# Layer 3 cross-attention: the order in which each unit's turns, score groups and sums are issued, and VectorE's order with it

## The chip, the cores and the metric

One core of a Trainium2 chip runs the whole program. The metric is the device time of one execution in microseconds (us): the kernel before has a median of 3372.61 us over 3 runs (3367.91 to 3373.32).

## The reference, cut to what matters

The program is a four-layer perceiver with 128 latent rows of width 256. The change touches one stage, the cross-attention of layer 3, whose main part is attention of 16 heads over all but the last 4 of 12,544 context rows of width 192:

```python
q = _split_heads(q_in)
k = _split_heads(k_in)
v = _split_heads(v_in)
s = jnp.einsum('bhid,bhjd->bhij', q, k) * SCALE
p = jax.nn.softmax(s, axis=-1)
o = jnp.einsum('bhij,bhjd->bhid', p, v)
```

## The kernel before, in words

The stage never builds keys or values. The key weights are folded into the queries, so a score is a product of a folded query (128 rows by 192) with a raw context row, and the softmax's weighted sum is taken over raw context rows; the value weights are applied afterwards by `finish_absorbed`. Each number is split into a high and a low fp32r part, so one product is several matmuls.

`absorbed_cross_attention` (line 1581) goes through 7 chunks of 1792 context rows, and in each through 16 heads: 112 **units** (`NU`), `u = 16 * chunk + head`. A unit has these steps:

- `raw_scores(u, s)`, s = 0 to 3 (lines 1607 to 1618), on TensorE: five matmuls of 448 columns (L1613 to L1617) into PSUM bank s % 2. The last signals `raw`. Two banks serve all groups, so group s waits (line 1611) for `maxed`, the end of VectorE's `keep` of the group two before.
- `keep(u, s)` (line 1694) on VectorE: L1701 copies the 448 scores out of PSUM into `raw[u % 2]`, with their maximum; the profile shows it as two instructions, the second reading the accumulator. It signals `maxed`.
- `new_max(u)` (line 1707) on VectorE: L1711 takes the maximum and signals `negmax`, L1715 stores it.
- `exp(u)` (line 1655) on ScalarE: two exponentials of 896 columns in place (L1661), each signalling `probs`, and the old sum's factor (L1663).
- `turn(u, gr)`, gr = 0, 1 (line 1620), on TensorE: seven 128x128 transposes (L1625) of a half into its own two PSUM banks. It waits for `probs` and signals `turned`.
- `keep_high(u, gr)` (L1669) on ScalarE copies a turned half rounded to fp32r; `keep_low(u, gr)` (L1720) on VectorE subtracts it from the turned half and signals `low`.
- `sums(u, gr)` (line 1629) on TensorE: fourteen matmuls (L1637 and L1638 in turn) against the context rows, into bank 6 or 7. It waits (line 1630) for `low` of its half.
- `take(u)` (L1726, L1729) on VectorE adds the unit's sums to the running ones, scaled by the factor.

Each engine's queue is in order and written out by hand. TensorE's order (lines 1642 to 1651) is, for each unit u: turn(u, 0), scores (u+1, 0) and (u+1, 1), turn(u, 1), scores (u+1, 2) and (u+1, 3), sums(u, 0), sums(u, 1). VectorE's (lines 1738 to 1747) is: keep_low(u, 0), keep(u+1, 0), keep(u+1, 1), take(u-1), keep_low(u, 1), keep(u+1, 2), keep(u+1, 3), new_max(u+1). ScalarE's is: keep_high(u, 0), keep_high(u, 1), exp(u+1). GpSimd splits the next chunk's context rows once per chunk and SyncE loads them; both are one chunk ahead.

Of the kernel before, what the change touches and what calls it, by code (L numbers as in the profile page):

```python
# [56 lines left out]
class Stage:  # L57
# [5 lines left out]
    def sem(self, name):  # L63
        if name not in self.sems:
            self.sems[name] = self.nc.alloc_semaphore(f"{self.tag}_{name}")
        return self.sems[name]
# [18 lines left out]
def at_least(eng, sem, value):  # L85

    if isinstance(value, int) and value <= 0:
        return
    eng.wait_ge(sem, value)
# [19 lines left out]
def bank(g, n, lo=0, hi=BANK):  # L109
    return g.ps[:, n * BANK + lo:n * BANK + hi]  # L110
# [1470 lines left out]
def absorbed_cross_attention(nc, g, a):  # L1581

    with ExitStack() as ctx:
# [9 lines left out]
        NU = NCH * H  # L1593

        def turned_banks(gr):
            return g.ps[:, (2 + 2 * gr) * BANK:(2 + 2 * gr) * BANK + GW]

        @block.sync
        def _(sp):
            for c in range(1, NCH):  # L1600
                if c >= 2:
                    sp.wait_ge(sem("split"), 6 * (c - 1))
                load_chunk(sp, g, a, c, sem("chunk"))

        @block.tensor
        def _(pe):
            def raw_scores(u, s):
                c, h = u // H, u % H
                if h == 0 and s == 0 and c > 0:
                    pe.wait_ge(sem("split"), 6 * c)  # L1610
                at_least(pe, sem("maxed"), 4 * u + s - 1)
                out, cols, p = bank(g, s % 2, 0, SUB), slice(s * SUB, s * SUB + SUB), c % 2
                pe.matmul(out, g.q_high[:, h, 0, :], g.high_a[:, p, cols], start=True, stop=False)  # L1613
                pe.matmul(out, g.q_high[:, h, 0, :], g.low_a[:, p, cols], start=False, stop=False)
                pe.matmul(out, g.q_low[:, h, 0, :], g.high_a[:, p, cols], start=False, stop=False)
                pe.matmul(out, g.q_high[:, h, 1, :], g.both_b[:, p, cols], start=False, stop=False)
                pe.matmul(out, g.q_low[:, h, 1, :], g.both_b[:, p, cols], start=False, stop=True)\  # L1617
                  .then_inc(sem("raw"), 1)

            def turn(u, gr):  # L1620
                pe.wait_ge(sem("probs"), 2 * u + gr + 1)
                at_least(pe, sem("low"), 2 * (u - 1) + gr + 1)
                for t in range(GT):
                    key = (gr * GT + t) * 128
                    last = pe.transpose(turned_banks(gr)[:, t * 128:t * 128 + 128], raw[u % 2][:, key:key + 128],  # L1625
                                        g.ident)
                last.then_inc(sem("turned"), 1)

            def sums(u, gr):
                pe.wait_ge(sem("low"), 2 * u + gr + 1)  # L1630
                if gr == 0:
                    at_least(pe, sem("taken"), u - 1)
                out = bank(g, 6 + u % 2, 0, TW)
                for t in range(GT):
                    tile, cols = gr * GT + t, slice(t * 128, t * 128 + 128)
                    rhs = g.tokens[:, u // H % 2, tile, :]
                    pe.matmul(out, high[gr][:, cols], rhs, start=(tile == 0), stop=False, skip_group_check=True)  # L1637
                    last = pe.matmul(out[:, 0:C + 2], low[gr][:, cols], rhs[:, 0:C + 2], start=False,  # L1638
                                     stop=(tile == TPC - 1), skip_group_check=True)
                last.then_inc(sem("sums"), 1)  # L1640

            for s in range(4):
                raw_scores(0, s)
            for u in range(NU):
                for gr in range(2):
                    turn(u, gr)
                    if u + 1 < NU:
                        raw_scores(u + 1, 2 * gr)
                        raw_scores(u + 1, 2 * gr + 1)
                sums(u, 0)  # L1650
                sums(u, 1)

# [39 lines left out]
        @block.vector  # L1692
        def _(dve):
            def keep(u, s):
                c, h = u // H, u % H
                last_keys = c == NCH - 1 and s == 3
                dve.wait_ge(sem("raw"), 4 * u + s + 1)
                if s == 0:
                    at_least(dve, sem("turned"), 2 * (u - 1))
                width = SUB - (IPA if last_keys else 0)  # L1700
                dve.tensor_scalar(raw[u % 2][:, s * SUB:s * SUB + width], bank(g, s % 2, 0, width), 0.0, None,  # L1701
                                  ALU.add, ALU.max, accum_out=tops[:, h, s:s + 1]).then_inc(sem("maxed"), 1)
                if last_keys:

                    dve.memset(raw[u % 2][:, CH - IPA:CH], -3e38)

            def new_max(u):
                c, h = u // H, u % H
                dve.wait_ge(sem("maxed"), 4 * u + 4)
                at_least(dve, sem("probs"), 2 * (u - 3))  # L1710
                dve.tensor_reduce(negmax[:, u % 4:u % 4 + 1], tops[:, h, :], AX.X, ALU.max, negate=True)\  # L1711
                   .then_inc(sem("negmax"), 1)
                dve.wait_ge(sem("negmax"), u + 1)
                old = 4 + (c + 1) % 2
                dve.tensor_scalar(tops[:, h, old:old + 1], negmax[:, u % 4:u % 4 + 1], -1.0, None, ALU.mult)\  # L1715
                   .then_inc(sem("top_kept"), 1)

            def keep_low(u, gr):
                dve.wait_ge(sem("high"), 2 * u + gr + 1)
                dve.tensor_tensor(low[gr][:], turned_banks(gr), high[gr][:], ALU.subtract).then_inc(sem("low"), 1)  # L1720

            def take(u):
                h, part = u % H, bank(g, 6 + u % 2, 0, TW)
                dve.wait_ge(sem("sums"), 2 * (u + 1))
                dve.wait_ge(sem("factor"), u + 1)
                dve.scalar_tensor_tensor(out=acc[:, h, :], in0=acc[:, h, :], scalar=factor[:, u % 4:u % 4 + 1],  # L1726
                                         in1=part[:, 0:CW], op0=ALU.mult, op1=ALU.add).then_inc(sem("scaled"), 1)
                dve.wait_ge(sem("scaled"), u + 1)
                dve.tensor_tensor(acc[:, h, 0:C], acc[:, h, 0:C], part[:, C + 2:TW], ALU.add)\  # L1729
                   .then_inc(sem("taken"), 1)  # L1730

            dve.memset(tops[:], -3e38).then_inc(sem("tops"), 1)
            dve.wait_ge(sem("tops"), 1)
            dve.wait_ge(sem("acc_zero"), 1)
            for s in range(4):
                keep(0, s)
            new_max(0)
            for u in range(NU):
                for gr in range(2):
                    keep_low(u, gr)  # L1740
                    if u + 1 < NU:
                        keep(u + 1, 2 * gr)
                        keep(u + 1, 2 * gr + 1)
                    if gr == 0 and u > 0:
                        take(u - 1)
                if u + 1 < NU:
                    new_max(u + 1)
            take(NU - 1)


# [1140 lines left out]
```

## Time and profile before

| | us |
|---|---|
| median of 3 runs | 3372.61 |
| the profiled execution | 3372.62 |
| its span in the trace | 3370.9 |

Over the whole span TensorE's matmuls are busy 2945.2 us (87%), VectorE 1830.0 us (54%), ScalarE 1350.9 us (40%). The units run from 2097 us to 3191 us of the span. In the trace PE is TensorE's matmuls and PEld its weight loads, which run beside them; DVE is VectorE and ACT is ScalarE. A line of the timeline gives the start, the duration, the engine, the line of the kernel, and how many like instructions were merged (x7: seven). A matmul's end is modelled and reaches past the start of the next, so TensorE's time is best read from start to start.

### The profile page before, as it was taken

The page shows a single profiled execution, that of the slowest core. Times are in us where ns is not written, and L with a number is a line of the kernel's source. Part 1 is how long each engine was busy: PE and PEld are TensorE (multiplying, and loading weights), DVE is VectorE, ACT ScalarE, POOL GpSimd, SP SyncE. Part 2 cuts the span into 40 slices and gives each one's busy share as a digit, 9 for nine tenths or more (in the row PEclk, how much of TensorE's full clock was granted, in tenths as well). Part 3 has the DMA queues.
Part 4 walks back from the last instruction along what each step waited for, and adds up shares of the span by engine and source line. Part 5 has one row for each costly group of instructions (what it writes and reads, how often), then busy time and mean ns, then how long its engine had stood idle before and what let it go on. Part 6 is the DMA issues. An engine that isn't in the chain of part 4 may idle for free. (4 is left out here: it accounts for less than half of the span.)

```text
span 3370.9 us, 66496 instructions
## 1 busy us (share of the span) xinstructions
PE 2945.2 (87%) x27158; PEld 2487.7 (74%) x27158; DVE 1830.0 (54%) x3246; ACT 1350.9 (40%) x2191; POOL 404.1 (12%) x571
## 2 busy tenths in 40 slices
PE   6999809998768999477999669999999999999978
PEld 6888706776564777463777455999999999999867
DVE  5555418774527775446776343555555555555524
ACT  4444305665003666123667120444444444444311
POOL 2443400000100000000000002220202020200000
PEclk9999958998787999686999685999999999999969
DMA  4898879882468883158884271100101010000016
GB/s 154 281 289 270 269 152 182 177 176 64 153 187 177 174 176 78 46 191 178 175 176 101 82 220 36 52 18 22 39 1 39 1 39 1 1 1 1 17 50 227
DMA packets 251093, 393.95 MB, mean 117 GB/s; under 512 B 45827, under 2 KB 214149, under 8 KB 250789
## 3 DMA queue, kind: packets, MB, share of 16 engines
q1 hardware_dynamic: 250791, 389.70, 45.3%
q8 instruction: 217, 3.56, 0.5%
q14 instruction: 85, 0.69, 0.1%
HBM read 289.45 MB, written 99.49 MB: 115 GB/s over the span
## 5 line engine op out<-in xcount | busy, mean ns | idle before, releaser
L712 DVE TENSOR_REDUCE L_xattn_tops<-psum 128x1 f32<-128x896 f32 x672 | 702.4, 1086 | 270.3 <-PE psum L564 269.1
L625 ACT ACTIVATE L_xattn_probs<-psum 128x512 f32<-128x512 f32 x1176 | 612.3, 600 | 518.2 <-PE psum L575 518.1
L1720 DVE TENSOR_TENSOR L_units_low<-psum,L_units_high 128x896 fp32r<-128x896 f32 x224 | 243.6, 1088 | 486.8 <-ACT L_units_high L1669 486.8
L564 PE MATMUL psum<-L_xattn_keys,L_xattn_q_stack 96*128 96x448 bf16 (+1 forms) x1344 | 395.2, 378 | 110.5 <-DMA L_xattn_q_stack<-query_parts 65.2
L1637 PE MATMUL psum<-wide_tokens,L_units_high 128*128 128x386 f32 x1568 | 456.5, 358 | 1.4 <-DVE L_units_low L1720 1.4
L575 PEld LDWEIGHTS psum<-L_xattn_q_stack,L_xattn_keys 99*128 99x128 bf16 (+1 forms) x4704 | 323.1, 98 | 144.4 <-issue 19.2
L575 PE MATMUL psum<-L_xattn_q_stack,L_xattn_keys 99*128 99x128 bf16 (+1 forms) x4704 | 394.2, 221 | 5.0 <-ACT L_xattn_probs L625 5.0
L1638 PE MATMUL psum<-wide_tokens,L_units_low 128*128 128x194 f32 x1568 | 395.1, 252 | 0.0
L588 PE MATMUL psum<-L_xattn_probs,L_xattn_values 128*17 128x128 f32 x9408 | 358.5, 277 | 0.2 <-issue 0.2
L1669 ACT CAST L_units_high<-psum 128x896 fp32r<-128x896 f32 x224 | 203.3, 908 | 363.7 <-PE psum L1625 363.7
L1661 ACT ACTIVATE L_units_raw<-L_units_raw,L_units_negmax 128x896 f32<-128x896 f32 x224 | 221.6, 1036 | 308.4 <-DVE L_units_negmax L1711 308.4
L1638 PEld LDWEIGHTS psum<-wide_tokens,L_units_low 128*128 128x128 f32 x1568 | 299.1, 191 | 1.7
L1637 PEld LDWEIGHTS psum<-wide_tokens,L_units_high 128*128 128x128 f32 x1568 | 294.9, 188 | 3.0 <-DVE L_units_low L1720 1.6
L588 PEld LDWEIGHTS psum<-L_xattn_probs,L_xattn_values 128*17 128x17 f32 x9408 | 260.7, 98 | 38.8 <-issue 1.1
L1701 DVE TENSOR_SCALAR_CACHE_REDUCE L_units_raw<-psum 128x448 f32<-128x448 f32 x448 | 259.7, 617 | 4.5 <-POOL wide_acc L1680 2.6
L564 PEld LDWEIGHTS psum<-L_xattn_keys,L_xattn_q_stack 96*128 96x128 bf16 (+1 forms) x1344 | 91.7, 100 | 220.9 <-issue 67.1
L1625 PE MATMUL psum<-band,L_units_raw 128*128 128x128 f32 x1568 | 207.9, 272 | 2.0 <-ACT L_units_raw L1661 2.0
L410 POOL TENSOR_TENSOR proj_parts<-proj_rest,proj_parts 128x896 bf16<-128x896 f32 x84 | 160.3, 1909 | 249.8 <-ACT proj_parts L328 249.8
L1625 PEld LDWEIGHTS psum<-band,L_units_raw 128*128 128x128 f32 x1568 | 179.9, 140 | 10.3 <-ACT L_units_raw L1661 2.4
L1613 PE MATMUL psum<-wide_high_a,wide_q_high 128*128 128x448 f32 x448 | 184.7, 412 | 2.2 <-PEq L78 2.2
L2578 PE MATMUL psum<-xnT,L_ffn_w 128*128 128x128 f32 x1056 | 141.3, 292 | 27.5 <-DMA L_ffn_w<-in_L_ffn_W 14.2
L2578 PEld LDWEIGHTS psum<-xnT,L_ffn_w 128*128 128x128 f32 x1056 | 137.3, 206 | 35.8 <-issue 14.2
(436 smaller groups left out, 3990.6 us busy)
## 6 DMA issues: line engine op xcount, KB each, us to landing
key_parts<-proj_parts SPq DMA_DIRECT2D x84, 672.0 KB, 5.1
L_xattn_keys<-key_parts SPq DMA_DIRECT2D x144, 336.0 KB, 4.7
values_scratch<-proj_values SPq DMA_DIRECT2D x18, 1904.0 KB, 11.9
L_xattn_values<-values_scratch SPq DMA_DIRECT2D x144, 238.0 KB, 5.4
L_ffn_w<-in_L_ffn_W SPq DMA_DIRECT2D x32, 1024.0 KB, 6.8
L_xattn_keys<-key_parts SPq DMA_DIRECT2D x144, 224.0 KB, 5.0
L_xattn_keys<-key_parts SPq DMA_DIRECT2D x192, 112.0 KB, 5.1
L_ffn_w<-in_L_ffn_w SPq DMA_DIRECT2D x16, 1024.0 KB, 6.3
```

The source lines that it names most:

```text
L564: last = pe.matmul(top_slot(n)[:, s, :], q_stack[0:P1, h, :], keys[0:P1, v % RING, key:key + WIN // 2], start=True, stop=True)
L575: last = pe.matmul(score_bank(k)[:, i * 128:i * 128 + 128], keys[0:P2, u % RING, key:key + 128], q_stack[0:P2, u // NCH, :], start=True, s ...
L588: last = pe.matmul(sum_bank[row:row + VW, :], values[:, u % RING, t, :], probs[:, at:at + 128], start=(c * TPC + t < 4), stop=(c * TPC + t ...
L625: act.activation(group_probs(k), score_bank(k), ACT.Exp).then_inc(sem("probs"), 1)
L712: dve.tensor_reduce(tops[:, h % 2, 2 * c + w:2 * c + w + 1], top_slot(n), AX.XY, ALU.max)\
L1625: last = pe.transpose(turned_banks(gr)[:, t * 128:t * 128 + 128], raw[u % 2][:, key:key + 128], g.ident)
L1637: pe.matmul(out, high[gr][:, cols], rhs, start=(tile == 0), stop=False, skip_group_check=True)
L1638: last = pe.matmul(out[:, 0:C + 2], low[gr][:, cols], rhs[:, 0:C + 2], start=False, stop=(tile == TPC - 1), skip_group_check=True)
L1661: act.activation(half, half, ACT.Exp, bias=new).then_inc(sem("probs"), 1)
L1701: dve.tensor_scalar(raw[u % 2][:, s * SUB:s * SUB + width], bank(g, s % 2, 0, width), 0.0, None, ALU.add, ALU.max, accum_out=tops[:, h, s: ...
L1720: dve.tensor_tensor(low[gr][:], turned_banks(gr), high[gr][:], ALU.subtract).then_inc(sem("low"), 1)
L2578: last = pe.matmul(bank(g, 2 * slot + half, j * T, j * T + T), buf[par][:, k, col:col + 128], g.xnT[:, k, :], start=(k == 0), stop=(k == D ...
```

## The change

TensorE issues both turns of unit u, then the four score groups of unit u+1, then the sums. VectorE's queue becomes: keep(u+1, 0), keep(u+1, 1), keep_low(u, 0), keep(u+1, 2), keep_low(u, 1), keep(u+1, 3), new_max(u+1), take(u-1). No instruction is added, removed or altered; the waits inside the steps stay as they are.

```diff
             for s in range(4):
                 raw_scores(0, s)
             for u in range(NU):
-                for gr in range(2):
-                    turn(u, gr)
-                    if u + 1 < NU:
-                        raw_scores(u + 1, 2 * gr)
-                        raw_scores(u + 1, 2 * gr + 1)
+                turn(u, 0)
+                turn(u, 1)
+                if u + 1 < NU:
+                    for s in range(4):
+                        raw_scores(u + 1, s)
                 sums(u, 0)
                 sums(u, 1)
...
             new_max(0)
             for u in range(NU):
-                for gr in range(2):
-                    keep_low(u, gr)
-                    if u + 1 < NU:
-                        keep(u + 1, 2 * gr)
-                        keep(u + 1, 2 * gr + 1)
-                    if gr == 0 and u > 0:
-                        take(u - 1)
-                if u + 1 < NU:
+                ahead = u + 1 < NU
+                if ahead:
+                    keep(u + 1, 0)
+                    keep(u + 1, 1)
+                keep_low(u, 0)
+                if ahead:
+                    keep(u + 1, 2)
+                keep_low(u, 1)
+                if ahead:
+                    keep(u + 1, 3)
                     new_max(u + 1)
+                if u > 0:
+                    take(u - 1)
             take(NU - 1)
```

## Rows read from the trace of the kernel before

**Rows 1.** The page's slices of the span: the granted TensorE clock in tenths.
```profile
PEclk9999958998787999686999685999999999999969
```

**Rows 2.** One stretch, from unit 0's first ScalarE copy to unit 111's: busy time by engine.
```profile
core 0: us, PE busy (x) PEld busy (x) DVE busy (x) ACT busy (x) POOL busy (x), PEclk, DMA share, GB/s
2106.81:3184.90 1078.09, 1078.09 (x6884) 1029.75 (x6883) 582.88 (x1568) 441.52 (x557) 116.43 (x36) 1.00 0.06 17
```

**Rows 3.** L1613, the first matmul of a score group, over all units: durations, count, starts.
```profile
L1613 PE MATMUL psum<-wide_high_a,wide_q_high x444: 360/406/477, 2106.5 to 3178.9; 128*128 128x448 f32 x148
```

**Rows 4.** Timeline of the matmuls through one unit, to the next unit's first turn.
```profile
2620.61 0.93 PE L1625 MATMUL psum<-band,L_units_raw 128*128 128x128 f32 x7
2621.29 0.45 PE L1613 MATMUL psum<-wide_high_a,wide_q_high 128*128 128x448 f32 x1
2621.58 0.36 PE L1614 MATMUL psum<-wide_low_a,wide_q_high 128*128 128x448 f32 x1
...
2622.18 0.36 PE L1617 MATMUL psum<-wide_both_b,wide_q_low 128*128 128x448 f32 x1
2622.38 0.36 PE L1613 MATMUL psum<-wide_high_a,wide_q_high 128*128 128x448 f32 x1
...
2623.38 0.93 PE L1625 MATMUL psum<-band,L_units_raw 128*128 128x128 f32 x7
2624.20 0.48 PE L1613 MATMUL psum<-wide_high_a,wide_q_high 128*128 128x448 f32 x1
2624.51 0.36 PE L1614 MATMUL psum<-wide_low_a,wide_q_high 128*128 128x448 f32 x1
...
2626.31 0.34 PE L1637 MATMUL psum<-wide_tokens,L_units_high 128*128 128x386 f32 x1
...
2630.32 0.93 PE L1625 MATMUL psum<-band,L_units_raw 128*128 128x128 f32 x7
```

**Rows 5.** Timeline of the weight loads of the same unit.
```profile
2621.26 0.19 PEld L1613 LDWEIGHTS psum<-wide_high_a,wide_q_high 128*128 128x128 f32 x1
2621.37 0.19 PEld L1614 LDWEIGHTS psum<-wide_low_a,wide_q_high 128*128 128x128 f32 x1
...
2622.18 0.19 PEld L1613 LDWEIGHTS psum<-wide_high_a,wide_q_high 128*128 128x128 f32 x1
...
2624.20 0.19 PEld L1613 LDWEIGHTS psum<-wide_high_a,wide_q_high 128*128 128x128 f32 x1
2624.30 0.19 PEld L1614 LDWEIGHTS psum<-wide_low_a,wide_q_high 128*128 128x128 f32 x1
```

**Rows 6.** Timeline of VectorE through the same unit.
```profile
2622.51 1.09 DVE L1720 TENSOR_TENSOR L_units_low<-psum,L_units_high 128x896 fp32r<-128x896 f32 x1 [4.34 <-ACT L_units_high L1669]
2623.52 0.61 DVE L1701 TENSOR_SCALAR_CACHE_REDUCE L_units_raw<-psum 128x448 f32<-128x448 f32 x1
2624.06 0.08 DVE L1701 DVE_READ_ACCUMULATOR L_units_raw<-psum 128x1 f32 x1
...
2624.60 0.41 DVE L1726 SCALAR_TENSOR_TENSOR wide_acc<-wide_acc,L_units_factor,psum 128x193 f32<-128x193 f32 x1
...
2626.86 0.62 DVE L1701 TENSOR_SCALAR_CACHE_REDUCE L_units_raw<-psum 128x448 f32<-128x448 f32 x1
...
2627.53 0.16 DVE L1711 TENSOR_REDUCE L_units_negmax<-L_units_tops 128x1 f32<-128x6 f32 x1
```

**Rows 7.** Timeline of ScalarE in the same unit.
```profile
2621.57 0.91 ACT L1669 CAST L_units_high<-psum 128x896 fp32r<-128x896 f32 x1 [1.39 <-PE psum L1625]
...
2627.72 1.98 ACT L1661 ACTIVATE L_units_raw<-L_units_raw,L_units_negmax 128x896 f32<-128x896 f32 x2 [2.46 <-DVE L_units_negmax L1711]
```

**Rows 8.** Timeline before the first unit, where VectorE waits for a score group.
```profile
2102.43 0.37 PE L1617 MATMUL psum<-wide_both_b,wide_q_low 128*128 128x448 f32 x1
...
2102.83 0.62 DVE L1701 TENSOR_SCALAR_CACHE_REDUCE L_units_raw<-psum 128x448 f32<-128x448 f32 x1 [0.80 <-PE psum L1617]
```

**Rows 9.** Timeline of the last unit, which has no score groups between its turns.
```profile
3183.93 1.70 PE L1625 MATMUL psum<-band,L_units_raw 128*128 128x128 f32 x14
...
3185.83 1.09 DVE L1720 TENSOR_TENSOR L_units_low<-psum,L_units_high 128x896 fp32r<-128x896 f32 x1 [4.37 <-ACT L_units_high L1669]
...
3186.98 0.44 PE L1637 MATMUL psum<-wide_tokens,L_units_high 128*128 128x386 f32 x1 [1.35 <-DVE L_units_low L1720]
```

## The prediction

> **What bounds the kernel now.** I read the page's slices first: the granted clock is 9 tenths or more through the slices that hold the units [rows 1], and the stretch from the first to the last unit has a granted clock of 1.00, the upper of the two levels, with TensorE busy for all of its 1078.09 us while VectorE is busy 582.88 and ScalarE 441.52 [rows 2]. So TensorE's queue sets the time, and no clock change is to be had. That stretch holds 111 periods: 1078.09 / 111 = 9.71 us a unit. A busy share of 100% says nothing of stalls, since matmul ends are modelled and cover small gaps; those are found in the timeline, from start to start. Every unit but the last issues four score groups for its successor, and the 444 first matmuls of such groups [rows 3] are 111 x 4.
>
> One unit on TensorE [rows 4]: from the first turn to the second 2.77 us, from the second turn to the sums 2.93, the sums 4.01, together 9.71. The two first pieces hold the same work, seven transposes and two score groups. A score group's five matmuls take 1.00: from L1614 to the next group's L1613, four matmuls on, are 0.80 (2621.58 to 2622.38), so 0.20 each. The first piece is therefore 0.77 + 2.00, the second 0.77 + 2.00 + **0.16 of stall**. The cause is in the queues: VectorE starts keep(u+1, 0) only behind keep_low(u, 0), which waits for ScalarE's copy; keep's accumulator read ends at 2624.06 + 0.08 = 2624.14 [rows 6], and the weight load of the third score group, which needs that PSUM bank, starts 0.06 later, at 2624.20 [rows 5]. In the undisturbed first piece this load comes 0.65 after the turn's first matmul (2621.26 against 2620.61), so it was due at 2624.03 and came 0.17 late. The same 0.06 between VectorE's end and TensorE's start stands in the last unit (3185.83 + 1.09 = 3186.92, then 3186.98) [rows 9].
>
> **The change, part by part.** I put T at the first turn's first matmul and work out the new unit.
>
> *TensorE.* The same instructions in another order. Fourteen transposes in one stretch are in the last unit already: 1.70 against 0.93 for seven, so the second seven cost 0.77 [rows 4, 9], as above; no switching cost disappears or appears. Scores 4 x 1.00, sums 4.01. Without stalls: 1.54 + 4.00 + 4.01 = 9.55 us. Score group 2's first matmul (L1613) is due at T + 0.77 + 2.77 = T + 3.54, group 3's at T + 4.54, the first sum at T + 5.54. The gain is the stall, 0.16, if nothing takes its place. What was freely early before now must be checked, because keep(u+1, 0), keep(u+1, 1) and keep_low(u, 0) each gate TensorE directly.
>
> *Gate 1, keep(u+1, 0) before score group 2.* The group's last matmul, L1617, starts 1.57 after its turn's first matmul [rows 4], so at T + 0.77 + 1.57 = T + 2.34. VectorE starts 0.40 after it when it is waiting (2102.43 to 2102.83) [rows 8], T + 2.74; the accumulator read ends 0.62 later (2623.52 to 2624.14) [rows 6], and with 0.06 the weight load is released at T + 3.42. Undisturbed it would go 0.20 before its matmul (2622.18 against 2622.38) [rows 4, 5], at T + 3.34. So it is 0.08 late. How much of that reaches the matmuls depends on how long a load needs: behind the stall, the next load starts 0.10 after the released one, and its matmul L1614 stands 0.31 after it, that is 0.10 of load and 0.20 of matmul [rows 4, 5]. A load released at T + 3.42 is ready at T + 3.52, before T + 3.54. Bounds: 0 lost (the load hides under the running matmul) and 0.08 (none of the lateness hides). I take 0, because the row with the 0.10 is the same load of the same line.
>
> *Gate 2, keep(u+1, 1) before group 3.* All of it is 1.00 later, so it loses nothing beyond gate 1.
>
> *Gate 3, keep_low(u, 0) before the sums.* It was done 2.7 us before the first sum (2622.51 + 1.09 = 2623.60, against 2626.31) [rows 4, 6]; now it is queued behind two keeps. keep(u+1, 1) starts at T + 3.74, the next VectorE instruction 0.54 after it (as 2623.52, 2624.06 and 2624.60) [rows 6], keep_low lasts 1.09 and with 0.06 the sums' load is released at T + 5.43, ready at T + 5.53; the sum is due at T + 5.54. A subtraction right behind a keep isn't in the trace. Below, its pitch is 0.54 as for the next keep and for take's first instruction; above, 0.67 as for L1711 (2626.86 to 2627.53), which waits on the keep itself [rows 6]. I take 0.54, since keep_low needs nothing of the keep. With 0.67 the sums come 0.12 late. Gates are absolute times, so the losses don't add: the unit loses the largest one.
>
> *The rest of the ring.* keep(u+1, 2) starts 1.01 behind keep_low's start (2622.51 to 2623.52), T + 5.29; keep_low(u, 1) at T + 5.83, released for sums(u, 1) at T + 6.98, due T + 7.35; keep(u+1, 3) T + 6.84; new_max 0.67 later; ScalarE's exponentials 0.19 behind that (2627.53 to 2627.72), T + 7.70, and 1.98 long [rows 6, 7]. With 0.06 the second turn is released at T + 9.74 and its load is due at T + 10.21: 0.47 to spare, 0.67 for the first turn. ScalarE's copies start 0.96 behind each turn's first matmul [rows 4, 7], so the first is ready at T + 1.87 and the second at about T + 2.7, before VectorE asks for either. take(u-1), moved to the end, fits the idle time from T + 7.9 to T + 12.3, and the sums it takes are complete shortly after T; its `taken` is next needed by sums(u+1, 0) at T + 15. Cost nothing. GpSimd and SyncE keep their waits on counts that TensorE reaches no later, and no transfer moves.
>
> *Ends.* Unit 111 has no scores, so both orders run alike; unit 0's second turn waits some 0.2 us for its exponential once.
>
> *Sum.* 111 x 0.16 = 17.8 us, less 0.2, less an allowance of 0.01 a unit for gates with a margin of 0.01 to 0.02 (1.1 us): 16.5. The profiled execution, 3372.62, is within 0.01 of the median. 3372.6 - 16.5 = **3356.1 us**, 0.5% faster.
>
> **A rule that speaks against it.** The Trainium skill (TensorE: Matmul & The Clock Gate, "The mechanism" under "Part 3: Packing small matmuls — row/col tiling") says that weight loads overlap matmuls in flight only where their row groups differ. Here every matmul uses all 128 rows; by that rule a late load would delay its matmul in full, and the result would be the first rival's 3364.8. The trace disagrees so far: loads start 0.20 before their own matmuls, beside the one before, and a pitch of 0.20 for 448 columns leaves no room for a serial 0.10.
>
> **The rivals.**
>
> *Late loads are passed on (chance 0.15).* The unit loses 0.08 to 0.09 of the 0.16; 111 x 0.07 = 7.8 us remain: **3364.8**. For it: three gates lie within 0.02 us of my limit, and one pitch is taken from another instruction. Against it: the 0.10 of the released load.
>
> *The stall comes back in full (0.10).* Either a released load starts only when the running matmul has drained (group 1's L1617 at T + 3.34 with a modelled 0.36, so the next at T + 3.70 in place of 3.54), or keep_low's pitch is 0.67 and a little more. Both cost 0.12 to 0.17 a unit: **3372.6**, no change. The stall of before doesn't exclude the first, since there the load began as the transposes ended.
>
> *VectorE's queue becomes the bound (0.04).* The place is keep_low(u, 0), behind two keeps and ahead of the sums. It decides from 0.17 us of further delay (0.16 of gain and the margin of 0.01), and can be measured as slower from 0.06 beyond. If the subtraction's pitch were doubled to 1.08, the sums would come 0.53 late: 111 x 0.37 = 41 us slower, **3414**. Against it: no VectorE row shows a pitch longer than the instruction itself by more than 0.06.
>
> *It does not do what it says (0.03).* If keep(u+1, 0) were held by something other than the order, the stall would remain, near **3372**. The 0.06 release speaks against it.
>
> **How the numbers follow.** Forecast 0.68 (3351 to 3361), rivals 0.15, 0.10, 0.04, 0.03. A measurement of this kernel can tell about 0.2% (6.7 us) from no change, so faster means below 3365.9. The first rival's 3364.8 lies on that line; I count two thirds of it and the partial losses as faster: faster 0.80, same 0.15, slower 0.05. The range: below, 0.16 and the runs' own 3 us of scatter, with a little for another run's level, 3350; above, the first rival and 3 us, 3368.
>
> **What would show it.** Right: a period of 9.55 to 9.57 from turn to turn; 14 merged transposes; L1613 of group 2 at T + 3.54; the sums at T + 5.54; keep_low(u, 0) 0.54 behind keep(u+1, 1); exponentials at about T + 7.7. Wrong: a longer start-to-start gap at group 2 (rival one or two), at the first sum (keep_low's pitch), or TensorE idle before the second turn (the ring).

## The result, and the profile after

The changed kernel has a median of 3362.97 us over 20 runs, the kernel before 3375.28 us over 20 runs beside them. The ratio is 0.9959, 95% interval 0.9949 to 0.9968: 0.41% faster, some 14 us. (One execution of the changed kernel took 9983.99 us, three times every other; it is left out of the ratio.) The forecast was 3356.1 us, 16.5 us below the kernel before, with a range of 3350 to 3368.

What counts for the prediction is the stage of the units. In the trace of the changed kernel, the first matmuls of the turns of unit 0 and of unit 111 (start, duration, engine, line, how many merged):

```profile
2110.99 1.92 PE L1625 MATMUL psum<-band,L_units_raw 128*128 128x128 f32 x14 [1.99 <-ACT L_units_raw L1661]
...
3174.39 1.69 PE L1625 MATMUL psum<-band,L_units_raw 128*128 128x128 f32 x14
```

The period, the time from one unit's first turn to the next unit's, is (3174.39 - 2110.99) / 111 = **9.58 us**, against 9.71 before; 1063.40 us in place of 1078.14, 14.7 us less (before: unit 0's first turn at 2105.79, unit 111's at 3183.93, the latter in [rows 9]). The spans of the two profiled executions, 3370.9 and 3362.0, differ by only 8.9. The granted clock over the stretch is 1.00 in both. Nothing in the stage took the rest: unit 0 merely began 5.2 us later, in a program that is identical up to there, and what follows the last turn took 0.6 us more (187.61 against 186.97): 14.7 - 5.2 - 0.6 = 8.9.

One unit of the timeline after, TensorE first. T is 2609.23; its counterpart is [rows 4]:

```profile
2609.23 1.70 PE L1625 MATMUL psum<-band,L_units_raw 128*128 128x128 f32 x14
...
2610.97 0.36 PE L1614 MATMUL psum<-wide_low_a,wide_q_high 128*128 128x448 f32 x1
...
2612.57 0.36 PE L1617 MATMUL psum<-wide_both_b,wide_q_low 128*128 128x448 f32 x1
2612.77 0.37 PE L1613 MATMUL psum<-wide_high_a,wide_q_high 128*128 128x448 f32 x1
...
2614.59 0.36 PE L1617 MATMUL psum<-wide_both_b,wide_q_low 128*128 128x448 f32 x1
...
2614.79 0.33 PE L1637 MATMUL psum<-wide_tokens,L_units_high 128*128 128x386 f32 x1
```

Score group 2 begins at T + 3.54 and the sums at T + 5.56; no gap of the kind between 2623.38 and 2624.51 in [rows 4] is left. The weight loads and VectorE in the same unit answer to [rows 5, 6]:

```profile
2611.58 0.19 PEld L1613 LDWEIGHTS psum<-wide_high_a,wide_q_high 128*128 128x128 f32 x1
...
2612.66 0.19 PEld L1613 LDWEIGHTS psum<-wide_high_a,wide_q_high 128*128 128x128 f32 x1
...
2614.66 0.19 PEld L1637 LDWEIGHTS psum<-wide_tokens,L_units_high 128*128 128x128 f32 x1
```

```profile
2611.97 0.63 DVE L1701 TENSOR_SCALAR_CACHE_REDUCE L_units_raw<-psum 128x448 f32<-128x448 f32 x1 [3.72 <-PE psum L1617]
...
2612.52 0.08 DVE L1701 DVE_READ_ACCUMULATOR L_units_raw<-psum 128x1 f32 x1
...
2612.97 0.62 DVE L1701 TENSOR_SCALAR_CACHE_REDUCE L_units_raw<-psum 128x448 f32<-128x448 f32 x1 [0.37 <-PE psum L1617]
...
2613.52 1.08 DVE L1720 TENSOR_TENSOR L_units_low<-psum,L_units_high 128x896 fp32r<-128x896 f32 x1
```

VectorE now waits for TensorE (3.72 us before keep 0, 0.37 before keep 1) where it waited for ScalarE before. keep 0 ends at 2612.60 and the load it holds starts at 2612.66. Group 1's own load stood at its matmul's start less 0.20; this one stands at 2612.66 for a matmul at 2612.77, so it is late by 0.09 (the previous matmul began at 2612.57), and yet the matmul is on time to 0.01. The same holds at the sums: keep_low ends at 2613.52 + 1.08 = 2614.60, the load starts at 2614.66, 0.07 late, the sum at 2614.79.

Averaged over units 1 to 110 (unit 0 once takes longer, in the changed kernel because its second turn waits 0.2 us for its exponential), the pieces of a unit are, in us from start to start:

| piece | before | after |
|---|---|---|
| turns and the lead-in to the first group's L1614 | 0.973 | 1.739 |
| L1614 of group 0 to group 1 | 1.004 | 1.004 |
| group 1 to group 2 (before: with the second turn) | 1.924 | 1.012 |
| group 2 to group 3 | 1.006 | 1.010 |
| group 3 to the first sum's L1638 | 0.979 | 0.986 |
| the rest of the sums | 3.827 | 3.828 |
| unit | 9.712 | 9.578 |

### The profile page after: what moved, and what is told of

Its sections match the earlier page's. It is cut to its first block and busy times, and to the rows that moved or that the text cites. A ratio compares the mean times of both kernels' runs of the same rounds, so it can differ in the third digit from the quotient of the medians.

```text
span 3362.0 us, 66496 instructions
## 1 busy us (share of the span) xinstructions
PE 2935.8 (87%) x27158; PEld 2475.1 (74%) x27158; DVE 1841.7 (55%) x3246; ACT 1340.0 (40%) x2191; POOL 403.4 (12%) x571
## 5 line engine op out<-in xcount | busy, mean ns | idle before, releaser
L1701 DVE TENSOR_SCALAR_CACHE_REDUCE L_units_raw<-psum 128x448 f32<-128x448 f32 x448 | 277.7, 620 | 461.8 <-PE psum L1617 459.2
L1638 PE MATMUL psum<-wide_tokens,L_units_low 128*128 128x194 f32 x1568 | 394.9, 252 | 0.0
L1638 PEld LDWEIGHTS psum<-wide_tokens,L_units_low 128*128 128x128 f32 x1568 | 299.3, 191 | 0.0
L1669 ACT CAST L_units_high<-psum 128x896 fp32r<-128x896 f32 x224 | 192.3, 910 | 76.2 <-PE psum L1625 76.1
L1625 PE MATMUL psum<-band,L_units_raw 128*128 128x128 f32 x1568 | 190.1, 272 | 2.0 <-ACT L_units_raw L1661 2.0
L1613 PE MATMUL psum<-wide_high_a,wide_q_high 128*128 128x448 f32 x448 | 173.8, 388 | 2.2 <-PEq L78 2.2
L1625 PEld LDWEIGHTS psum<-band,L_units_raw 128*128 128x128 f32 x1568 | 172.8, 140 | 2.6 <-ACT L_units_raw L1661 2.6
```

## The experiments

**e1.** The changed kernel again, on the chip of the next three.

> The changed kernel once more, to be compared with the three others on one chip. Both theories: 9.58 us from turn to turn (the trace of after), 14.8 us below the kernel before.

Measured: 3367.11 us, ratio to the kernel before 0.9953 (0.9937 to 0.997). Its unit 0 turns at 2114.86 and unit 111 at 3177.81: a period of 9.58. It is the yardstick for e2 to e4, which ran on that chip; the kernel before has a median of 3383.18 us there. In the stretch of the units the granted clock is 1.00 in every run below.

**e2.** VectorE's new order, TensorE's old one. The edit is shown against the changed kernel:

```diff
             for u in range(NU):
-                turn(u, 0)
-                turn(u, 1)
-                if u + 1 < NU:
-                    for s in range(4):
-                        raw_scores(u + 1, s)
+                for gr in range(2):
+                    turn(u, gr)
+                    if u + 1 < NU:
+                        raw_scores(u + 1, 2 * gr)
+                        raw_scores(u + 1, 2 * gr + 1)
```

> VectorE's new order with TensorE's old one. Theory (the gain is the stall of the third score group, held by keep(u+1, 0) behind keep_low(u, 0)): keep(u+1, 0) starts about T + 1.97, the second turn's groups are released long before they are due, no gate is late, and the period is 9.56 us, 111 x 0.155 = 17 us below before and some 2.5 us below after. Rival (the gain comes from the turns and the groups in one stretch on TensorE): 9.71 us, no change.

Measured: 3369.98 us, ratio 0.9959 (0.9947 to 0.9971). The timeline around the second turn, to be held against [rows 4, 6]:

```profile
2622.09 0.62 DVE L1701 TENSOR_SCALAR_CACHE_REDUCE L_units_raw<-psum 128x448 f32<-128x448 f32 x1 [3.48 <-PE psum L1617]
...
2622.89 0.93 PE L1625 MATMUL psum<-band,L_units_raw 128*128 128x128 f32 x7
...
2623.86 0.36 PE L1614 MATMUL psum<-wide_low_a,wide_q_high 128*128 128x448 f32 x1
```

keep(u+1, 0) is over before the second turn starts, and L1614 follows that turn by 0.97, as it follows the first, in place of 1.13. The piece that measured 1.924 before is 1.773 here, and the period 9.56, as expected (unit 0 at 2113.14, unit 111 at 3174.65: 1061.51 / 111). VectorE's order alone brings all of the gain. The rival, that the stretches on TensorE bring it, falls. The run times don't show that e2 is shorter than the changed kernel: its median lies 2.9 us above e1's where 2.5 us below were expected, and the intervals of the two ratios overlap. Only the periods tell the two apart.

**e3.** The other half: TensorE's new order with VectorE's queue of the kernel before. The edit, again against the changed kernel, begins with:

```diff
-                ahead = u + 1 < NU
-                if ahead:
-                    keep(u + 1, 0)
-                    keep(u + 1, 1)
-                keep_low(u, 0)
...
+                for gr in range(2):
+                    keep_low(u, gr)
+                    if u + 1 < NU:
+                        keep(u + 1, 2 * gr)
+                        keep(u + 1, 2 * gr + 1)
+                    if gr == 0 and u > 0:
+                        take(u - 1)
...
```

> TensorE's new order with VectorE's old one. Theory: keep(u+1, 0) starts behind keep_low(u, 0) at T + 2.88, the load of group 2 is released at T + 3.56 and due at T + 3.34, 0.10 of that is hidden: a stall of 0.12, period 9.68 us, 3 to 5 us below before. Rival (one stretch on TensorE is the gain): 9.56 to 9.58 us, as after.

Measured: 3386.06 us, ratio 1.0005 (0.9996 to 1.0014): nothing gained. Period 9.71 (2122.34 to 3200.62: 1078.28 / 111), where I expected 9.68. In the timeline:

```profile
2630.45 0.62 DVE L1701 TENSOR_SCALAR_CACHE_REDUCE L_units_raw<-psum 128x448 f32<-128x448 f32 x1
2630.88 0.37 PE L1617 MATMUL psum<-wide_both_b,wide_q_low 128*128 128x448 f32 x1
2630.99 0.08 DVE L1701 DVE_READ_ACCUMULATOR L_units_raw<-psum 128x1 f32 x1
2631.13 0.47 PE L1613 MATMUL psum<-wide_high_a,wide_q_high 128*128 128x448 f32 x1
...
2631.43 0.37 PE L1614 MATMUL psum<-wide_low_a,wide_q_high 128*128 128x448 f32 x1
```

```profile
2631.12 0.19 PEld L1613 LDWEIGHTS psum<-wide_high_a,wide_q_high 128*128 128x128 f32 x1 [0.25 <-DVE L_units_raw L1701]
```

keep is again behind keep_low, its load comes at 2631.12, 0.24 after its place at the previous matmul's start (2630.88), and group 1 to group 2 takes 1.156 in place of 1.004: 0.15 lost. The stall has only moved from the second turn to the middle of the score groups. TensorE's order by itself gains nothing.

**e4.** The kernel before with one pair of VectorE's instructions exchanged:

```diff
                 for gr in range(2):
+                    if u + 1 < NU and gr == 0:
+                        keep(u + 1, 0)
                     keep_low(u, gr)
                     if u + 1 < NU:
-                        keep(u + 1, 2 * gr)
+                        if gr == 1:
+                            keep(u + 1, 2)
                         keep(u + 1, 2 * gr + 1)
```

> The kernel before with one instruction pair exchanged in VectorE's queue: keep(u+1, 0) ahead of keep_low(u, 0) (and, as it stands, keep(u+1, 2) behind keep_low(u, 1) as before). Theory: keep(u+1, 0) at T + 1.97, keep_low(u, 0) at T + 2.5, the stall is gone, period 9.56 us, 17 us below before, as e2. Rival: 9.71 us.

Measured: 3366.84 us, ratio 0.9951 (0.9937 to 0.9965). Period 9.56 (2117.67 to 3179.18: 1061.51 / 111), the piece across the second turn 1.773:

```profile
2626.61 0.62 DVE L1701 TENSOR_SCALAR_CACHE_REDUCE L_units_raw<-psum 128x448 f32<-128x448 f32 x1 [4.18 <-PE psum L1617]
...
2627.16 1.08 DVE L1720 TENSOR_TENSOR L_units_low<-psum,L_units_high 128x896 fp32r<-128x896 f32 x1
...
2627.41 0.93 PE L1625 MATMUL psum<-band,L_units_raw 128*128 128x128 f32 x7
...
2628.38 0.36 PE L1614 MATMUL psum<-wide_low_a,wide_q_high 128*128 128x448 f32 x1
```

keep(u+1, 0) runs ahead of keep_low(u, 0), and L1614 follows the second turn by 0.97. take stays in the middle, and keep(u+1, 1) stays behind keep_low(u, 0). One exchange does what the whole change does, and against e1 nothing in the run times sets them apart (3366.84 and 3367.11); in the traces it is 0.01 us a unit shorter.

**e5.** The changed kernel with a small fill ahead of keep_low, to measure how near to its limit the sums' wait is:

```diff
                     keep(u + 1, 1)
+                    dve.memset(pad[:], 0.0)
                 keep_low(u, 0)
```

Here `pad` has 4 columns.

> The changed kernel with a fill of 128x4 elements in VectorE's queue between keep(u+1, 1) and keep_low(u, 0). In the trace of after the sums' first weight load is already about 0.09 us later than its place and the sums lose under 0.01. Theory (a late load costs its lateness less 0.09): whatever start delay d the fill gives keep_low (0.06 to 0.11 expected) is passed on in full, period 9.58 + d, 9.64 to 9.69 us. Rival (a late load waits until the running matmul has drained, a fixed step): a step of about 0.17 whatever d is. Rival (keep_low was not at its limit): 9.58.

Measured: one run, 3357.15 us; period 9.58 (2104.44 to 3167.72: 1063.28 / 111). The fill was to delay keep_low by 0.06 to 0.11 and did so by 0.01: it starts 0.56 behind the keep (2625.59 and 2626.15) where it started 0.55 behind it. My expectation of the delay was wrong, and the run therefore doesn't tell the theory from its rivals.

**e6.** The same with 192 columns.

> The same with a fill of 128x192 elements, which should delay keep_low by some 0.2 to 0.3 us (128x96 took 0.14 us). Theory: again passed on one for one, period 9.58 + d, 9.78 to 9.88 us. Rival (fixed step): no more than e5 by the difference of the steps, i.e. about 9.75 in both.

Measured: one run, 3372.22 us; period 9.71 (2106.73 to 3184.31: 1077.58 / 111), less than the 9.78 to 9.88 expected, because the fill of 0.22 us delays the end of keep_low by 0.15 only. The lines of the kernel are one further down than in the others (L1702 is keep, L1721 keep_low, L1638 the first sum):

```profile
2625.11 0.63 DVE L1702 TENSOR_SCALAR_CACHE_REDUCE L_units_raw<-psum 128x448 f32<-128x448 f32 x1 [0.38 <-PE psum L1618]
...
2625.73 0.22 DVE L1744 MEMSET L_units_pad<- 128x192 f32 x1
2625.86 1.03 DVE L1721 TENSOR_TENSOR L_units_low<-psum,L_units_high 128x896 fp32r<-128x896 f32 x1
...
2626.72 0.37 PE L1618 MATMUL psum<-wide_both_b,wide_q_low 128*128 128x448 f32 x1
...
2626.95 0.19 PEld L1638 LDWEIGHTS psum<-wide_tokens,L_units_high 128*128 128x128 f32 x1 [0.23 <-DVE L_units_low L1721]
```

keep_low ends at 2626.89, 1.78 behind keep's start, against 1.63 after (2612.97 to 2614.60): d is 0.15. The load comes at 2626.95, 0.23 after its place at 2626.72, and group 3 to the first sum takes 1.107 in place of the undisturbed 0.979: 0.13 lost. Of the lateness 0.10 is hidden and the rest is paid. A fixed step for any late load, as if the running matmul had first to drain, would have shown in the changed kernel already, where three loads are 0.07 to 0.09 late, and didn't. The traces also speak against a fixed step for loads that are later than that, since the units of one trace differ a little: in e6 the quarter of the units with the smallest lateness (0.213 on average) loses 0.118 and the quarter with the largest (0.230) 0.134. No run has a load between 0.10 and 0.20 late behind a matmul of 448 columns, so where between them the loss begins is not shown.

**e7.** The kernel before with the fill of 192 columns between keep_low(u, 0) and keep(u+1, 0).

```diff
                     keep_low(u, gr)
+                    if gr == 0:
+                        dve.memset(pad[:], 0.0)
```

> The kernel before with a fill of 128x192 elements between keep_low(u, 0) and keep(u+1, 0), some 0.2 to 0.3 us. Theory (the stall is keep's lateness): the second turn's first score group waits longer by the same d, period 9.71 + d, 9.91 to 10.01 us, the gap L1614 to L1614 across the second turn 1.92 + d. Rival (the stall has another cause): 9.71.

Measured: one run, 3393.45 us; period 9.87 (2106.19 to 3201.61: 1095.42 / 111), 0.16 longer than before, where 9.91 to 10.01 was expected, again since the fill delays less than its length. In the trace (lines one further down, as in e6):

```profile
2621.26 1.09 DVE L1721 TENSOR_TENSOR L_units_low<-psum,L_units_high 128x896 fp32r<-128x896 f32 x1 [4.36 <-ACT L_units_high L1670]
...
2622.97 0.08 DVE L1702 DVE_READ_ACCUMULATOR L_units_raw<-psum 128x1 f32 x1
...
2623.10 0.19 PEld L1614 LDWEIGHTS psum<-wide_high_a,wide_q_high 128*128 128x128 f32 x1 [0.28 <-DVE L_units_raw L1702]
```

keep_low starts at 2621.26 and keep's accumulator read ends at 2622.97 + 0.08 = 2623.05, 1.79 later, against 1.63 before (2622.51 to 2624.14) [rows 6]: d is 0.16. The piece across the second turn grew from 1.924 to 2.080, by 0.156. The stall follows keep one for one, and the rival, another cause and a period of 9.71, falls.

**e8.** take put back into the middle of VectorE's unit:

```diff
                 keep_low(u, 0)
+                if u > 0:
+                    take(u - 1)
                 if ahead:
                     keep(u + 1, 2)
...
                     new_max(u + 1)
-                if u > 0:
-                    take(u - 1)
             take(NU - 1)
```

> The changed kernel with take(u-1) moved from the end of VectorE's unit to behind keep_low(u, 0), 0.72 us earlier than keep(u+1, 2). Theory (TensorE needs keep_low(u, 1) at about T + 7.45 and the ring has 0.47 to spare): keep_low(u, 1) ends 0.72 later, at about T + 7.64, the second half of the sums waits some 0.23, period 9.81 us, 25 us slower than after, 10 us slower than before. Rival (the place of take is free): 9.58.

Measured: 3385.06 us, ratio to the kernel before 1.003 (1.0013 to 1.0046), that is 10 us slower than before, as worked out; period 9.81 (2111.59 to 3200.36: 1088.77 / 111). The middle of the sums:

```profile
2629.02 1.08 DVE L1720 TENSOR_TENSOR L_units_low<-psum,L_units_high 128x896 fp32r<-128x896 f32 x1
...
2630.16 0.19 PEld L1637 LDWEIGHTS psum<-wide_tokens,L_units_high 128*128 128x128 f32 x1 [0.21 <-DVE L_units_low L1720]
```

The second half of the sums waits for keep_low(u, 1), 0.22 a unit; the remaining 1.5 us of the stage fall on unit 0 alone, which took 11.26 us. In the changed kernel take can't stand in this place; with e4's order it stands in the middle and costs nothing.

## Why the prediction was right, point by point

**The bound and the stall: right.** I read 0.16 of stall in each second turn and put it down to keep(u+1, 0) behind keep_low(u, 0). e4 removes only that order and takes the piece from 1.924 to 1.773, as e2 does with VectorE's whole new queue; e7 lengthens keep's delay by 0.16 and the piece by 0.156. The term was 0.150, not 0.16: 111 x 0.01 = 1.1 us of the forecast was rounding of rows with two decimals. The load that was read as 0.17 late in one unit is 0.15 late on average (it starts 0.810 behind the second turn's first matmul, and 0.658 in e4), so the whole of its lateness is the stall.

**TensorE's reordering adds nothing: right.** Fourteen transposes take what two times seven take; the turns with the lead-in to the first group's L1614 take 1.739, which is 0.973 and another 0.766. e3 shows the stretch alone to gain nothing.

**The gates: right in time, small in price, but the losses add.** Forecast against T = 2609.23: group 2's load T + 3.42, measured 3.43; its matmul 3.54 and 3.54; keep_low with a pitch of 0.54, measured 0.55; the sums' load 5.43 and 5.43, the sum 5.54 and 5.56. The allowance was 0.01 a unit. Measured against e2 (units 1 to 110), whose loads are on time, the pieces of the changed kernel that end in group 2, in group 3 and in the first sum are 0.005, 0.005 and 0.008 longer, the sums 0.001 shorter, and the unit 0.0156 longer: 1.7 us in all, for an allowance of 1.1. The prediction held that gates are absolute times, so that a unit loses only the largest of its losses. The traces don't bear that out at this size: the three small losses add up to the whole. No run has two large ones in one unit.

**The rest of the ring: right in the main.** The exponentials were due at T + 7.70:

```profile
2616.92 1.98 ACT L1661 ACTIVATE L_units_raw<-L_units_raw,L_units_negmax 128x896 f32<-128x896 f32 x2 [5.01 <-DVE L_units_negmax L1711]
```

They start at T + 7.69 and hold up no turn after unit 0. One due time was read wrong: the load for the second half of the sums is due at T + 7.45 (2616.68 in the trace after) and not at T + 7.35, because behind a matmul of 194 columns a load goes 0.09 ahead of its matmul and not 0.20. The margin was on the safe side. e8 was worked out from the right one before it ran: it adds 0.72 to the chain, 0.23 a unit was expected, and the sums lose 0.22.

**The sum.** Stage: forecast 17.8 - 0.2 - 1.1 = 16.5 us, measured 14.7 in the trace and 11 to 17 in the run times. The terms that were off are small, about 0.01 us a unit each: 1.2 us of stall (16.6 in place of 17.8) and 0.6 us of gates. The period of 9.58 therefore lies 0.01 above the 9.55 to 9.57 that were to show the forecast right. The level moved too: the kernel before has a median of 3375.28 over all its runs, not 3372.6, which accounts for 2.7 of the 6.9 us between 3356.1 and 3362.97. Of the rest, 1.8 are the two terms, and 2.4 are the difference between the 14.7 of the trace and the 12.3 between the two medians, for which no run shows a cause; the run times of either kernel scatter by more than that.

**The rivals.** Late loads passed on: by the run time alone this rival (3364.8) lies nearer to the 3362.97 than the forecast of 3356.1 does, so it is the period that decides. It would have been 9.64 and was 9.58, and in e3 and e6 0.09 to 0.10 of a late load is free behind a 448-column matmul. The rule of the Trainium skill (TensorE: Matmul & The Clock Gate, "The mechanism" under "Part 3: Packing small matmuls — row/col tiling"), by which loads overlap matmuls in flight only with other row groups, does not describe this trace: these loads use the same rows and overlap. The opening of that section of the Trainium skill also lets a load into the background weight buffer go ahead, which the prediction left out; no run here shows which buffer a load takes. Stall back in full: no drain step was seen, and keep_low's pitch was 0.55, not 0.67. VectorE as the bound: I put its threshold at 0.17 of further delay, and e6, with 0.15, has lost the gain and lands at the period of before. It does not do what it says: e4 and e7 show that the order held keep(u+1, 0).

## What to carry to other kernels

Before reordering a long unit, find the one wait that ends late, and ask what stands ahead of the late instruction in its own queue: here an independent subtraction waiting for another engine stood ahead of the copy that frees a PSUM bank, and exchanging the two gave all of the gain. Write down for each gate when it is released and when it is due; a larger rearrangement with the same effect used up nearly all margins (one more move, e8, turned 0.4% of gain into 0.3% of loss), while the small one kept the loads on time. At this size, compare periods in the trace, since the run times here didn't separate versions 0.1% apart (e1, e2 and e4).

## What the runs showed of the hardware that I had not expected

How much of a late weight load was free differed with the matmul in front of it. Behind a matmul of 448 columns 0.24 late cost 0.15 (e3) and 0.23 cost 0.13 (e6); behind the sums' shorter one (194 columns) nearly all was paid, 0.22 on average for 0.22 (e8; in the unit shown the load came at 2630.16 and was due at about 2629.93), and behind transposes all of it: 0.15 late cost 0.15 in the kernel before and 0.31 late cost 0.31 in e7, both held against e4. Within e8 the cost grows with the lateness one for one: the quarter of the units with the smallest lateness (0.198) loses 0.193, the quarter with the largest (0.240) 0.235.

A fill between two VectorE instructions cost less than its duration: 0.06 us of fill delayed the end of the next by 0.01 (e5), and 0.22 of fill by 0.15 to 0.16 (e6, e7), where in e6 keep_low began while the fill was running and was itself shorter by 0.05. In e5 the profile even puts the fill's start (2626.18) behind that of keep_low (2626.15), which the queue has behind it.

The part of the program ahead of the units is the same in all kernels, and yet the first turn fell between 2104.4 and 2111.6 us of the span in the traces of one chip (e5 to e8) and between 2113.1 and 2122.3 in those of the other (e1 to e4). Across chips that is more than the whole gain, and is why run times on different chips (3357.15 for e5's one run, a median of 3367.11 for e1, with the same period) say little here.
